# Next block's K projection planned ahead of the receptance matmuls in a fused attention and channel-mix layer (8 cores)

## What is computed

```python
x = x + _layernorm(attn(_layernorm(x), Wq, bq, Wk, bk, Wv, bv, Wo, bo))
x = x + _layernorm(ffn(_layernorm(x), W_r, W_k, W_v, mu_r, mu_k))
# attn: q, k, v projections, rope on q and k over the whole feature axis, 16 heads of 64,
#       each 512-token block attends to itself and the block before inside a band of 512, then Wo
# ffn:  xr, xk = mixes of x with x of the token before; 
#       out = sigmoid(xr @ W_r) * (relu(xk @ W_k)**2 @ W_v)
```

## Time and profile before

| what | value |
|---|---|
| median of 2 runs, slowest core | 5758.8 us |
| the profiled execution | 5776.13 us |
| its span on the slowest core (core 5) | 5774.5 us |
| spans of the 8 cores | 5739.8 to 5774.5 us |
| PE busy | 3249.5 us (56%) |
| DVE busy | 2473.3 us (43%) |
| ACT busy | 2120.3 us (37%) |
| POOL busy | 1201.0 us (21%) |
| mean granted TensorE clock, core 5 | 0.688 |

### The profile page before, as it was taken

The page is one execution under the profiler, slowest core; times in us unless marked ns, Lnnn a source line. Parts: engine busy times, 40 slices in busy tenths (PEclk is TensorE's granted clock), DMA queues, the critical chain, the costliest instruction groups (busy, mean ns, idle before and its releaser), DMA issues.

```text
span 5774.5 us, 52620 instructions; the slowest of 8 cores (5739.8 to 5774.5 us)
## 1 busy us (share of the span) xinstructions
PE 3249.5 (56%) x11840; PEld 1249.9 (22%) x11840; DVE 2473.3 (43%) x3561; ACT 2120.3 (37%) x3905; POOL 1201.0 (21%) x1028
## 2 busy tenths in 40 slices
PE   0355636657463674737745464674737467464673
PEld 0112212222121221212212121221212122121221
DVE  2353433444345343443535344343443544334342
ACT  0052532525323262442623344262442425344262
POOL 0011212222112121221311222121221212122122
PEclk9957568575675857668576765857658575765857
DMA  6603123131221303113031311303113130311301
GB/s 194 163 29 84 48 68 93 32 85 44 82 79 50 111 8 95 59 59 102 10 100 51 102 59 44 117 5 98 59 56 105 44 107 10 102 59 44 117 1 65
DMA packets 269845, 410.38 MB, mean 71 GB/s; under 512 B 151778, under 2 KB 151778, under 8 KB 269540
## 3 DMA queue, kind: packets, MB, share of 16 engines
q1 hardware_dynamic: 203492, 197.28, 13.4%
q0 software_dynamic: 33792, 134.22, 7.4%
q10 hardware_dynamic: 32256, 75.51, 3.4%
HBM read 297.89 MB, written 75.50 MB: 65 GB/s over the span
## 4 chain that ended last, share of the span: by engine, by line
PE 27%; DVE 22%; ACT 21%; DMA 8%; issue 8%; POOL 8%; SPq 3%; ACTq 2%; DVEq 1%; POOLq 0%
PE pb L521 8%; ACT pk L495 6%; PE pb L488 5%; DVE ybuf L533 4%; SPq L174 3%; ACT krot L250 3%; ACT krot L253 3%; DMA sinb<-sind 3%; PE pb L408 3%; PE pb L675 3%; PE pb L326 3%; DVE ax L637 3%; POOL ybuf L755 3%; PE pb L580 3%; POOL pk L713 2%
## 5 line engine op out<-in xcount | busy, mean ns | idle before, releaser
L533 DVE RECIPROCAL ybuf<-pb 1x512 bf16<-1x512 f32 x256 | 858.1, 3352 | 805.7 <-PE pb L521 797.3
L495 ACT ACTIVATE pk<-pb,neg 128x512 bf16<-128x512 f32 (+3 forms) x1792 | 945.3, 527 | 282.7 <-PE pb L488 27.4
L675 PE MATMUL pb<-WS,qx 128*128 128x512 bf16 x1024 | 297.7, 456 | 1200.7 <-DVE qx L644 981.1
L488 PE MATMUL pb<-qx,krot 64*128 64x512 bf16 (+3 forms) x1792 | 682.5, 435 | 393.6 <-ACT pk L495 307.6
L521 PE MATMUL pb<-pk,vext 128*65 128x128 bf16 (+3 forms) x2368 | 523.8, 404 | 79.1 <-DVE ax L546 33.1
L510 POOL TENSOR_TENSOR pk<-pk,tri4s 128x512 bf16<-128x512 bf16 x256 | 294.2, 1149 | 761.4 <-ACT pk L495 761.4
L506 POOL TENSOR_TENSOR pk<-pk,tri0s 128x512 bf16<-128x512 bf16 x192 | 220.8, 1150 | 1053.7 <-ACT pk L495 1053.7
L675 PEld LDWEIGHTS pb<-WS,qx 128*128 128x128 bf16 x1024 | 111.1, 113 | 1384.0 <-issue 1316.6
L326 PE MATMUL pb<-vext,Wwq 128*128 128x512 bf16 x1024 | 262.2, 418 | 243.1 <-DVE scr L350 243.1
L326 PE MATMUL pb<-vext,Wwk 128*128 128x512 bf16 x1024 | 241.1, 393 | 269.4 <-DMA vext<-hstage 226.5
L730 PE MATMUL pb<-WS,pk 128*128 128x512 bf16 x1024 | 294.0, 455 | 158.9 <-DVE pk L741 71.2
(11 more groups left out here) (105 smaller groups left out, 3857.1 us busy)
## 6 DMA issues: line engine op xcount, KB each, us to landing
xsl<-x SPq DMA_DIRECT2D x128, 512.0 KB, 3.9
WS<-wo_bf POOLq DMA_DIRECT2D x16, 2048.0 KB, 13.0
WS<-wr_bf POOLq DMA_DIRECT2D x16, 2048.0 KB, 22.5
cosb<-cosd SPq DMA_DIRECT2D x128, 256.0 KB, 5.2
sinb<-sind SPq DMA_DIRECT2D x128, 256.0 KB, 5.7
WS<-wk_bf POOLq DMA_DIRECT2D x16, 2048.0 KB, 10.5
WS<-wv_bf POOLq DMA_DIRECT2D x16, 2048.0 KB, 11.0
out<-ybuf ACTq DMA_DIRECT2D x64, 512.0 KB, 2.7
```

Of the source, the lines that this page charges most:

```text
L488: qlo=qlo, qhi=qhi: e.matmul(pb[bk][:, qlo:qhi], ksrc[po:po + 64, BS * md + 128 * tc:BS * md + 128 * (tc + 1)], qx[po:po + 64, BS * md + q ...
L495: texp = cop("scalar", lambda e, bk=bk, c=c, qlo=qlo, qhi=qhi, pku=pku: e.activation(out=pku[:, BS * c + qlo:BS * c + qhi], in_=pb[bk][:, ...
L533: t_rc = cop("vector", lambda e, rb=recipb[uslot], ub=ub: e.reciprocal(rb, pb[ub][64:65, :]), waits=[t_av, buf.get(("recip", uslot)), prev ...
L675: ins = e.matmul(pb[bk][:, :], qx[:, BS * ci + 128 * tj:BS * ci + 128 * (tj + 1)], WS[1][:, D * ci + BS * hh:D * ci + BS * (hh + 1)], star ...
```

## The change

The call of planB1 for the next block is moved from behind the R block to ahead of it. planA keeps its place. Nothing is added or taken away.

```diff
         if it + 1 < niter:
             pendingA = planA(it + 1, t_av_last)
 
+        if it + 1 < niter:
+            pendingB = planB1(it + 1, pendingA, buf.get("lnstat"))
+
         wr_users = []
         t_rsg = []
         for tj in range(4):
...
                 bank_free[bk] = trs
-
-        if it + 1 < niter:
-            pendingB = planB1(it + 1, pendingA, buf.get("lnstat"))
 
         t_wv2 = stream_weight("wv2", 1, wr_users)
```

## The result

The changed kernel is slower: 1.0501 times the kernel before, with a 95% interval of 1.0469 to 1.0533. The median is 6059.15 us over 11 runs; the profiled execution took 6057.84 us. The forecast was 6054 us, range 6025 to 6090. Some executions of both kernels had one die at a lower granted clock; the ratios here leave them out.

A forecast was written before the change was run, and what follows sets the result against it. No engine is near full; the transposes' landing paces the transitions, then one chain follows. 19.34 + 2.2 - 1.2 - 0.7 = 19.6 us, times 15 = 295 us on 5776.1 = 6071, by the median 6054; range 6025 to 6090.

The forecast's parts named there:

- Bound: At block transitions the transposes' landing sets the pace; the R block runs meanwhile, costing nothing or 1 to 2 us each.
- 1, the R block: R block, now between K projection and k block, adds 19.34 us per transition to the path; 20.9 with a cold pair.
- 2: K projection's first matmul pair starts cold after PE's idle time: +2.2 us per transition (+1.4 to +2.9).
- 3: K projection starts earlier, no longer queued behind the R block: -1.2 us per transition, bounds 0 and 4.0.
- 4: Slow K projection stretches, from late sine tiles and a lower granted clock, go away: -0.7 us per transition.
- 5, the stream of wv2: The wv2 load waits for the R block but stays covered by the k block: cost nothing, 6.7 us of cover left.
- The rival: The wv2 stream takes 22.5 us, so the v2 block waits 4.8 us more per transition: 6126 us; chance 0.04.
- The rival of the clock: R, k and neighbours run without full clock, at block 0's level: 6.0 us more per transition, 6144 us; chance 0.06.
- 6, sigmoids and relus: Sigmoids keep their place on ACT, relus wait for the k block anyway, VectorE's rope is done in time: nothing.
- One sign: If the forecast is right, the k block starts 41 to 42 us after the landing, against 21 to 24 before.
- The swallowing rival: The next rope of q's sine tile wait absorbs up to 16.1 of the 19.6 us: 5811 us; chance 0.03.

The follow-up runs named there:

- the cut: R block left with 2 of 8 matmuls per group: kernel before with wv2's stream held, 0.9971 of before; changed kernel, 1.0269 of before.
- after_preload: Changed kernel plus one ScalarE sigmoid over constants behind planA, loading the sigmoid table ahead; 1.0417 of the kernel before.
- after_warm_late: Changed kernel plus 52 filler matmuls ahead of planB1, released by the landing of the store to hstage; mean span 6024.4 us against 6038.1.
- r_last_pair: Kernel before with only the last of the four R pairs moved behind planB1; 1.0123 of the kernel before.
- 8 fillers: Changed kernel plus 8 filler matmuls ahead of planB1, released by planA's last normalised tile; 1.0459 of the kernel before.
- after_warm: Changed kernel plus 52 filler matmuls ahead of planB1, released by planA's last normalised tile; 1.0572 of the kernel before.

## Why the prediction was right, point by point

**Bound.** That the landing sets the pace and the R block was hidden is shown by the cut: 0.9971 in the old order with the stream held, and 1.0501 to 1.0269 in the new one. To be exact, PE was still in the R block for 1.0 us (core 5) to 2.2 us (core 2) after the landing in the mean, which is the 1 to 2 us of the prediction.

**1, the R block: 19.34 us forecast, 20.2 measured** (19.7 to 20.5 on the six cores). All of it on the path. The term is 0.9 us short: I said PE would be at full clock since it comes from matmuls. It is, in the first pair; but it fell in the second, after the table load's wait, in 54 of 90 transitions (R to k block is 19.2 or 20.9 us, seldom between). I had the 5.15 us pair of the last block as upper end for a cold first pair, and looked at the wrong pair. The slow second pair could have been read ahead of the run: the last block of the kernel before has it on core 3, where my rows came from core 5 alone.

```profile
5676.76 5.30 PE L675 MATMUL pb<-WS,qx 128*128 128x512 bf16 x16 [2.12 <-ACT qx L686]
```

after_preload shows that without the long wait it does not come; after_warm_late, with 16 of 90 behind the same wait, shows that the wait alone does not decide it. What else does stays open.

**2, 3 and 4, the K projection: +2.2 - 1.2 - 0.7 = +0.3 forecast, +0.2 measured.** The first pair took 5.4 to 5.8 us in the mean of each core, 2.0 more than the 3.62 before. The projection started 0.25 us behind the landing instead of 1.6 (1.0 on core 5, from which my rows came, 1.8 and 2.2 on cores 1 and 2): -1.3. That cold matmuls are what rope waits for is shown by after_warm_late. Of the slow K stretches 0.5 us went and not 0.7: 0.4 between the first pair and rope, where the late sine tile had stood, and 0.1 behind it. In the pieces of the table this is the +0.3 from landing to rope and -0.1 of what stands at +20.1. That wv2's move did it was not tested alone.

**5, the stream of wv2: nothing forecast, nothing measured.** The v2 block waits 3.04 us for POOL's square, as in the earlier trace rows, and k to v2 block is 17.1. The rival is out.

**The rival of the clock.** The Trainium skill's rule on the peak-current limit ("TensorE: Matmul & The Clock Gate", Part 1) did not decide this case: in the profiled execution R and k block took 3.61 us per pair wherever the clock had not fallen after a wait, and the k block's 64 matmuls 14.1 us in every block of the six cores. By the figure of 1.95 GHz that the Trainium skill gives there, the estimate for 128 matmuls is 6.3 us; the prediction's 6.0 is what its rows give (8 pairs at 0.75 us). A pair of 4.36 us does appear in a run of another order (r_last_pair on die 1), so the level exists outside block 0.

**6, sigmoids and relus: nothing, and so it is.** VectorE's first multiply of the v2 block waits for PE (567.0 us, against 300.5), not for rope.

**The sum.** 19.6 us per transition forecast, 18.9 measured; 295 us against 284. That it comes so near is in part luck: R was 0.9 too small, and 1.4 us per turn came back in pieces that I had at zero (landing -0.7, rope of q to V -0.4, and two small ones), so the two errors cancel. One sign was missed by this: the k block starts 42.7 us after the landing (6.0 + 36.7), not 41 to 42. The swallowing rival is out: the wait for the sine tile moved along, and the 38 us from v2 block to rope of q stayed.

## What to carry to other kernels

Where engines run lists in order, a block of work that stands ahead of a late operand is free until the operand comes, and the same block behind it costs its full length; so ask of each reordering which side of the latest wait it puts the work on. Work that fits into the waits behind the operand (the q step between the K steps) is the move that pays. A block's end may also release a large transfer: making it shorter can start that transfer on top of a more urgent one, as wv2 on the transposes.

## What the runs showed of the hardware that was not expected

A 2 MB stream issued in the middle of eight DMA transposes delayed their landing by 6.8 us per transition; holding the stream back took that away.

TensorE's granted clock fell behind a wait of 2.12 us in 54 of 90 R blocks, and in none of 90 behind the wait of 0.84 us in the same place (after_preload): the pair took 5.30 us and not 3.61. With fillers up to the K projection (after_warm_late) it fell in 16 of 90 behind the same 2.12 us. The changed kernel's stretches on core 5 at transition 2, where that pair begins at 895.66, show it at 0.50 of 2.4 GHz, which is 1.2 GHz:

```profile
872.00:896.00 24.00, 19.30 (x87) 8.29 (x86) 17.54 (x24) 2.27 (x3) 0.00 (x0) 0.99 0.27 68
896.50:899.90 3.40, 3.40 (x9) 1.21 (x8) 0.00 (x0) 0.00 (x0) 0.00 (x0) 0.50 0.35 114
```

With 52 fillers the landing came later: 16.8 and 16.4 us from the last tile, against 15.8 with 8 fillers or none. In after_warm 0.7 of the 1.0 us lies ahead of the transposes: the last store to hstage, which ran beside the fillers, landed 3.0 us after its issue ended, and 2.3 to 2.4 in the other runs. In after_warm_late the store is as fast as ever, and the eight transposes take 10.6 us to issue instead of 10.1. What causes either stays open. The 16.5 us of the kernel before are a mean of 15.9 to 16.0 on cores 1, 2 and 4 and 16.7 to 17.2 on cores 3, 5 and 7, and the cut R block with the stream held still had 16.4, so matmuls beside the transposes are not shown to be the reason there.
